# A decoder's causal attentions: the triangle of the maxima moves from VectorE's operand to added matmuls on TensorE

## The reference, cut

```python
x = _layernorm(x + _L0_attn_ref(x, ...))       # causal, heads normed, rotated
x = _layernorm(x + _L0_xattn_ref(x, ctx, ...)) # cross attention to 1601 keys, with a mask
x = _layernorm(x + _L0_ffn_ref(x, ...))        # one fp8 product
x = _layernorm(x + _L1_attn_ref(x, ...))       # causal attention and an MLP
x = _layernorm(x + _L1_xattn_ref(x, ctx, ...)) # cross attention, no mask
x = _layernorm(x + _L1_ffn_ref(x, ...))        # mixture of experts, two of eight
# within the causal attentions, for each head:
scores = scale * einsum('bhqd,bhkd->bhqk', q, k)     # then -inf where key > query
out = einsum('bhqk,bhkd->bhqd', softmax(scores), v)
```

## Time and profile before

| | us |
|---|---|
| median of 3 runs | 3051.54 |
| lowest and highest run | 3050.11, 3053.46 |
| the profiled execution's own time | 3052.74 |
| its span | 3051.0 |

### The profile page before, as it was taken

One profiled execution on the slowest core, in us unless ns is written; L12 is line 12 of the kernel. 1 busy time (PEld: TensorE's weight loads), 2 busy tenths in 40 slices (PEclk: granted clock), 3 DMA queues, 4 the chain that ended last, 5 costly groups with the idle time before them and its releaser, 6 DMA issues. The chain is left out here.

```text
span 3051.0 us, 93944 instructions
## 1 busy us (share of the span) xinstructions
PE 2817.6 (92%) x39186; PEld 1046.2 (34%) x39187; DVE 2171.2 (71%) x6062; ACT 1824.3 (60%) x2158; POOL 542.7 (18%) x760
## 2 busy tenths in 40 slices
PE   4999999999999999967999998999999999899997
PEld 2522222522222222233222224652222222256664
DVE  7688986587878887565899993158888888652114
ACT  2388878436666666734588886234777777831222
POOL 0188870110000000001222113111000000002330
PEclk7899999979999999978899999997999999999999
DMA  3345541301110001102111112020111111111112
GB/s 98 111 130 131 135 111 35 118 18 25 25 26 25 17 24 26 36 20 76 33 47 43 42 45 83 1 74 23 39 52 52 52 53 32 35 58 62 44 43 86
DMA packets 120407, 166.79 MB, mean 55 GB/s; under 512 B 38227, under 2 KB 89310, under 8 KB 119984
## 3 DMA queue, kind: packets, MB, share of 16 engines
q1 hardware_dynamic: 102192, 117.21, 14.3%
q0 software_dynamic: 12320, 43.02, 4.6%
q10 hardware_dynamic: 5472, 0.56, 0.2%
HBM read 126.51 MB, written 26.72 MB: 50 GB/s over the span
## 5 line engine op out<-in xcount | busy, mean ns | idle before, releaser
L737 DVE TENSOR_REDUCE mpart<-ps 128x1 f32<-128x512 f32 (+2 forms) x1792 | 1014.2, 616 | 149.2 <-PE ps L548 148.1
L548 PE MATMUL ps<-stack 48*32 48x401 f16 (+5 forms) x13312 | 987.9, 355 | 55.3 <-DVE mpart L737 25.3
L475 ACT ACTIVATE xT<-ps,exp_scale 128x1024 f32<-128x1024 f32 (+3 forms) x800 | 794.6, 1028 | 284.6 <-PE ps L569 137.5
L475 ACT ACTIVATE cn<-ps,exp_scale 128x1024 f32<-128x1024 f32 (+4 forms) x800 | 743.1, 959 | 233.6 <-PE ps L569 119.7
L569 PE MATMUL ps<-stack 50*32 50x512 f16 (+3 forms) x11648 | 744.4, 377 | 56.2 <-ACT xT L475 42.3
L548 PEld LDWEIGHTS ps<-stack 48*32 48x32 f16 x13312 | 293.3, 91 | 1056.6 <-DVE mpart L737 562.8
L733 DVE CUSTOM_DVE_ANT_0 scrap<-ps,arena 128x401 bf16<-128x401 f32 (+1 forms) x1024 | 534.3, 574 | 128.0 <-PE ps L548 128.0
L609 PE MATMUL ps<-xT,vall 128*17 128x512 f32 (+4 forms) x3648 | 422.5, 524 | 2.2 <-POOL xT L434 1.4
L609 PE MATMUL ps<-cn,vall 128*17 128x512 f32 (+3 forms) x3392 | 412.9, 508 | 1.0 <-ACT cn L475 1.0
L569 PEld LDWEIGHTS ps<-stack 50*32 50x32 f16 x11648 | 194.6, 91 | 209.2 <-ACT xT L475 110.5
L727 DVE CUSTOM_DVE_ANT_0 scrap<-ps,scrap 128x128 bf16<-128x128 f32 (+3 forms) x512 | 247.6, 485 | 19.7 <-PE ps L548 15.1
(11 more groups left out here) (281 smaller groups left out, 2510.9 us busy)
## 6 DMA issues: line engine op xcount, KB each, us to landing
stack<-q_parts SPq DMA_DIRECT2D x384, 64.0 KB, 2.6
stack<-k_parts SPq DMA_DIRECT2D x192, 64.0 KB, 2.9
wbuf<-in_maskT POOLq DMA_DIRECT2D x24, 512.0 KB, 4.7
arena<-in_moe_w SPq DMA_DIRECT2D x19, 512.0 KB, 4.4
stack<-k_parts SPq DMA_DIRECT2D x192, 50.0 KB, 2.3
stack<-sums_inverse SPq DMA_DIRECT2D x16, 512.0 KB, 5.6
parts<-osb SPq DMA_DIRECT2D x240, 32.0 KB
wbuf<-in_mask POOLq DMA_DIRECT2D x16, 401.0 KB, 4.0
```

Of the source, the lines that this page charges most:

```text
L475: nc.scalar.activation(e.prob[tile % P_SLOTS][0:rows, half * HALF + first:(half + 1) * HALF], S_PS(g)[0:rows, first:HALF], ACT.Exp, scale= ...
L548: last = nc.tensor.matmul(bank[quarter(j), 0:w], qs[b][rows, t * P + 32 * j:t * P + 32 * j + 32], ks[b][rows, a:a + w], start=True, stop=True)
L737: nc.vector.tensor_reduce(dst, src, AX, ALU.max).then_inc(unit_used, 1)
```

## The change

Three things are changed.

- In `unit` on PE, a diagonal unit's four matmuls leave their accumulation open, and four more follow, with 64 rows (the same half of the array as the unit's own), 32 columns and 128 columns of data: the identity times the triangle `above16`, added to the last 128 keys of the unit's bank. `unit_ready` is raised by the last of these.
- In `unit` on DVE, a diagonal unit is a plain `tensor_reduce` like every other; the wait on `unit_used` ahead of it, the scratch write, and the tile of zeros and triangle in `scrap` (L832, L833, twice in the program) are gone.
- `LEAST_UP` is 1 in place of 2^-9, so `to_powers` no longer gives a factor that makes products larger. `rope_phase` loads the upper triangle in two halves of 64 rows (two more DMAs in the list `later` on SP) and casts it to `above16` (one more DVE instruction, 128x256).

```diff
-LEAST_UP = 2.0 ** -9
+LEAST_UP = 1.0
@@ attention_phase, PE
                     for j in range(4):
                         last = nc.tensor.matmul(bank[quarter(j), 0:w], qs[b][rows, t * P + 32 * j:t * P + 32 * j + 32],
-                                                ks[b][rows, a:a + w], start=True, stop=True)
+                                                ks[b][rows, a:a + w], start=True, stop=not diagonal)
+                    if diagonal:
+                        for j in range(4):
+                            own = first + 32 * (j % 2)
+                            last = nc.tensor.matmul(bank[quarter(j), w - P:w], e.ident16[first:first + ROWS, own:own + 32],
+                                                    e.above16[first:first + ROWS, j // 2, :], start=False, stop=True)
                     last.then_inc(unit_ready, 1)
@@ attention_phase, DVE
-                    if diagonal:
-                        if g >= 3:
-                            dve.wait_ge(unit_used, g - 2)
-                        nc.vector.tensor_tensor_reduce(out=e.scrap[:, t % 3, 0:w], in0=src, in1=e.scrap[:, 3, CH - w:CH],
-                                                       scale=1.0, scalar=-3.0e38, op0=ALU.add, op1=ALU.max,
-                                                       accum_out=dst).then_inc(unit_used, 1)
-                    elif masked:
+                    if masked:
...
-                if causal:
-                    nc.vector.memset(e.scrap[:, 3, 0:CH - P], 0.0).then_inc(diagonal_set, 1)
-                    nc.vector.tensor_copy(e.scrap[:, 3, CH - P:], e.upper16).then_inc(diagonal_set, 1)
@@ rope_phase
-        later += [(wide[g * ROWS:(g + 1) * ROWS, 2 * P:].rearrange("p (k c) -> p k c", k=2),
-                   e.d["lower"].rearrange("(k p) c -> p k c", k=2)) for g in range(2)]
+        later += [(wide[g * ROWS:(g + 1) * ROWS, (2 + 2 * i) * P:(4 + 2 * i) * P].rearrange("p (k c) -> p k c", k=2),
+                   e.d[n].rearrange("(k p) c -> p k c", k=2)) for g in range(2) for i, n in enumerate(("lower", "upper"))]
...
-                nc.vector.tensor_copy(e.lower16.rearrange("p k c -> p (k c)"), wide[:, 2 * P:])
+                nc.vector.tensor_copy(e.lower16.rearrange("p k c -> p (k c)"), wide[:, 2 * P:4 * P])
+                nc.vector.tensor_copy(e.above16.rearrange("p k c -> p (k c)"), wide[:, 4 * P:])
```

More of the change, by code:

```diff
@@ L176, in attention_phase @@
         pads_set = sem("pads_set") if keys % P else None
-        diagonal_set = sem("diagonal_set") if causal else None
         sums_in, rec_made, rec_out, scaled = sem("sums_in"), sem("rec_made"), sem("rec_out"), sem("scaled")
@@ L840, in _ @@
                 dve.wait_ge(parts_set, 4)
-                if causal:
-                    dve.wait_ge(diagonal_set, 2)
                 for u in range(nu):
@@ L905, in rope_phase @@
     ROW = G * 2 * D
-    with phase(nc) as sem, nc.sbuf_tensor(f"turning_{nc.next_id()}", [P, 4 * ROW + 4 * P], F32) as turning:
+    with phase(nc) as sem, nc.sbuf_tensor(f"turning_{nc.next_id()}", [P, 4 * ROW + 6 * P], F32) as turning:
         w_in, small_in, later_in, whole = sem("w_in"), sem("small_in"), sem("later_in"), sem("whole")
@@ L2023, in build @@
         e.upper16, e.lower16 = sb("upper16", P, BF16), sb("lower16", 2 * P, BF16).rearrange("p (k c) -> p k c", k=2)
+        e.above16 = sb("above16", 2 * P, BF16).rearrange("p (k c) -> p k c", k=2)
         e.bounds, e.up, e.down = (sb(n, 8).rearrange("p (i a) -> p i a", i=2) for n in ("bounds", "up", "down"))
```

## The result

| | before | after |
|---|---|---|
| median, us (15 runs each) | 3052.97 | 3059.42 |
| lowest and highest run | 3046.11, 3056.28 | 3055.80, 3066.37 |
| profiled execution, its span | 3052.74, 3051.0 | 3060.34, 3058.6 |

The changed kernel takes 1.0025 of the time of before, with an interval of 1.0017 to 1.0033: some 7.6 us more, 6.5 by the medians. A second measurement of the same two kernels gave 1.0025 again, 1.0015 to 1.0035. So it is slower: the intervals leave out 1, but the step is a quarter of a per cent. The forecast was 9.8 us more.

What follows compares the result with a forecast made beforehand. PE, DVE and ACT were all taken as near their limit, none alone the bound. PE's 0.42 us a head less DVE's 0.1, times 30, gave 9.6 us; plus 0.2 on 3051.5 made 3061.3 us, range 3047 to 3076.

Steps and rivals of the forecast that it cites:

- narrow slots: Four diagonal units up to the turn, where PE sets the pace: all four pay, 0.24 us a head.
- The price of four matmuls: On PE, four added matmuls cost 0.06 us per diagonal unit, read from the same step in the first attention's scores.
- rival 4: Weight load exposed behind the unit's own matmuls: 0.15 us per diagonal unit, 28.5 us in all, 3080; chance 0.03.
- The count of those on the path: 7 of a head's 16 diagonal units delay it, 0.42 us a head, the same number taken for both attentions.
- the turn: Place in a head where a wait for ACT and 1.49 us without DVE work follow; its diagonal unit costs none.
- the dense stretch: 1604.61 to 1614.20, where DVE sets the pace: one of four diagonal units pays; as long as before or 0.05 us shorter.
- The credit for DVE: Plain maxima gain 0.01 us per diagonal unit, about 0.1 us a head for some nine units in DVE's own stretches.
- the equal starts: On DVE, read-out and next maximum both start at 1605.22, so the 83 ns read-out lies beside its successor's fill.
- a product of 30 with a head's difference: A head's change comes some 15 times in each causal attention: 30 x 0.32 = 9.6 us.
- The cross-check: First attention already has 16 such groups a head and is 0.50 us longer than the second: 30 times gives 15 us.
- The edges: Outside the heads' loop: units ahead of it 0, rope phase's added cast 0.2 us, DMAs, memset and `LEAST_UP` 0.
- rival 1: PE pays nearly all: 11 to 16 of 16 count, dense stretch longer, 17 to 29 us more, 3068 to 3080; chance 0.2.

Runs made afterwards that it cites:

- pe_alone: The kernel after with DVE's custom instruction kept in the diagonal units, so PE's half only (both add the triangle); ratio 1.0039 to before.
- dense_only: The kernel after with the change in the four diagonal units of tiles 12 to 15 alone, the others as before; ratio 0.9999 to before.
- dve_alone: The kernel after without the four added matmuls, so DVE's plain maxima only, the triangle left out of the maxima; ratio 0.9985 to before.
- The memsets: Two runs: the kernel before with one or two DVE memsets behind each diagonal unit of tiles 12 to 15; ratios 1.0018 and 1.0053 to before.
- edges: The kernel before with only the changed `LEAST_UP` and the rope phase of after (two more DMAs, one more cast); ratio 0.9997 to before.
- rows128: The kernel after with the triangle added by four matmuls over all 128 rows of the array, not the unit's 64-row half; ratio 1.0267 to before.

## Why the prediction was right, and where it was off

- *The sign and the mechanism* were right. PE's pace in the narrow slots went from 1.06 to 1.12 us, as written, and the product from 0.26 to 0.33 us after the diagonal unit (0.32 forecast).
- *The price of four matmuls*, 0.06 us, carried over from L575 to L552. The load of weights was not in the open (rival 4): the step begins 0.17 us after a unit of 384 columns, and its loads stand beside the unit. The Trainium skill's sentence in "TensorE: Matmul & The Clock Gate", "Part 3: Packing small matmuls", that a load overlaps matmuls in flight only when the row group differs, is not what this row shows. It would have made heads 0.95 us longer by the prediction's own working.
- *The count of those on the path*, 7 of 16, was 7 in the second attention (0.42 us in pe_alone) and 8 in the first (0.49). In the second each place can be read from DVE's starts, pe_alone against before (units counted from 0): none in the first four, 0.22 by unit 13, 0.28 by unit 14, of which 0.25 is left behind the turn, 0.12 at the 256-key unit after it and 0.05 to 0.06 each with the 512- and the 128-key unit behind it, with 0.06 taken back between them. So the narrow slots and the turn paid 0.25 where 0.24 was forecast, the places after the turn about two, the dense stretch one. In the first attention the sum was nearly right, but the places were not: 0.16 is lost by unit 7, none from there to unit 15, 0.17 at units 16 and 17, 0.06 by unit 23, and 0.11 in the dense stretch. dense_only measured 0.16 us there, where one of four, 0.06, was forecast; half of that shows at the start of a head, before its own changed units.
- *The credit for DVE*, 0.1 us a head, was mis-sized. It was 0.03 to 0.07 us (dve_alone), and 0.03 to 0.04 on top of PE's half (pe_alone less after). The read-out is free, as the equal starts said. On top of PE's half, 0.03 us comes in the dense stretch, nearly the 0.01 for each of its four units; the other five of the nine that were counted gave next to nothing. The memsets show slack of about that size, and more of it in the first attention, where dve_alone gained less. This term, and the eighth place in the first attention, made the heads 0.46 and 0.38 us longer where 0.32 was forecast.
- *From heads to time*: a product of 30 with a head's difference assumed that nothing else in the attentions moves. With the measured heads it gives 12.6 us, and 7.6 came. The mean clock was higher, and in the first attention its stretches at 1.2 GHz were rarer; that gave the rest back. The forecast of 9.8 us stands between, so two errors of 3 and 5 us, of opposite sign, met in it: that the number came as near as it did is luck. Nothing in the prediction looked at the heads that are not the commonest, though before's first attention has four of 26 us and more.
- *The cross-check*, 0.50 us between the attentions' heads, came nearer to 0.46 than the sum did; by the commonest heads it is 0.43. It deserved more weight than to confirm a sign.
- *The edges* can't be told from zero, within 0.2% (edges); the cast's 0.2 us shows in the trace.
- *The dense stretch* came out 0.03 us longer, where as long or 0.05 shorter was written: rival 1's sign of a longer one is there, but far from the 4 x 0.06 us that it would have been with every unit paid.

## What to carry to other kernels

Work that is added to the engine which sets the pace in only part of a loop costs its price times the places where it is late. Their number can be estimated from the starts in one period, but two loops of the same order need a count each; the whole period of after, and not the busy time, confirms it. Work taken from the other engine gives next to nothing as long as that engine has slack: lengthen its stretch and see what reaches the period before counting on a gain, and measure what was added from one unit to the next, not at the instruction behind it. A period times its count is not yet the time: here a higher mean clock gave back some 5 of 12.6 us. When small matmuls are added between others, keep them in the mode that their neighbours have.

## What the runs showed of the hardware beyond the forecast

- A change between a step of 64 rows and one of 128 costs about 0.10 us each way (0.27 against 0.17 us into it, 0.17 against 0.06 out of it), and 1.85 to 2.77 us a head of 25 us when each diagonal unit makes it.
- With PE busy some 95% of the time, the granted clock still falls to 1.2 GHz for single short stretches, 0 to 4 in 365 us, differing from one execution of the same kernel to the next (4, 2 and 1 for before). They begin right behind a microsecond in which PE was idle at the turn of a head, behind some turns and not behind others as long; each costs a head 1.2 to 1.5 us. rows128 had none between the first and last head of its first attention and 7 there in its second, four of them of double length: a head there takes 28.59 us at a mean clock of 0.88, against 26.21 at 1.00.

```profile
1664.15:1690.36 26.21, 25.12 (x503) 7.77 (x502) 22.61 (x45) 20.32 (x26) 6.05 (x18) 1.00 0.17 39
...
1716.58:1745.17 28.59, 27.53 (x505) 7.93 (x504) 22.80 (x46) 20.43 (x26) 6.05 (x18) 0.88 0.14 36
```

- A memset of 128 elements behind DVE's read-out starts 0.06 us after it, though a maximum starts beside it. With a duration of 0.17 us it moves the next start by 0.13 us and costs 0.06 us: the maximum behind it is 0.06 us shorter by starts. A second memset costs 0.12 us more.
